# Folding the output projection into the expert weights earlier, in another PSUM bank, with a new order of all stages

## The chip, the cores and the metric

The kernel runs on one core of a Trainium2 chip. The metric is the device time of one execution in microseconds (us), lower is better. The core has five engines that run side by side and meet only through semaphores: TensorE (PE, matrix products, writes PSUM), VectorE (DVE), ScalarE (ACT), GpSimd (POOL, which doesn't touch PSUM here) and SyncE (SP, which issues the DMAs). PSUM has 8 banks of 128 partitions x 512 float32.

## The reference

Two transformer layers on 8 sequences of 128 tokens, model width 128, float32. Cut to what matters:

```
x  = LN(x) attends over the context (77 rows), plus x           # front, "p1"
h  = LN(x)                                                      # "ln1"
Q, K, V = h @ q_w, h @ k_w, h @ v_w         # 16 heads, 4 numbers each in Q, K and V
A  = softmax(Q K^T / 2) V                   # [tokens, 64]
mla = A @ o_w[0:64] + o_b
probs = softmax(mla @ router_w + router_b); keep the top 2 of 8 experts
moe = sum_e combine_e * (gelu(mla @ w1[e] + b1[e]) @ w2[e] + b2[e])
x  = x + h + 0.3 * moe                      # then a second layer: "p4" (cross attention), "p5" (expert 7)
```

`mla` is used only as a factor of `router_w` and of `w1[e]`. The kernel never forms it: it computes `o_w @ w1[e]` for the eight experts ("fold", 128x2048 in all) and `o_w @ router_w` ("fr"), and multiplies `A` with these. `o_b` rides along as one more row.

## The kernel before

**Stages and order.** Every engine runs its own function with named stages. A table of some 800 words, `plan`, gives one order of all stages; `run` walks it on each engine and executes the stages which that engine has. So the order of a word against words of the same engine is the order of the engine's queue, which is strict; between engines only semaphores count. A word like `s1:2,0` is a stage with its arguments (sequence 2, group 0).

**Front.** The 8 sequences go through it in three units u of 2, 3 and 3. For each: `p1_stats`, `p1_norm`, `p1_T` (transpose on PE), `p1_scores`, `p1_soft` (exponentials on ACT), `p1_pT`, `p1_av` (context attention, then added to x by DVE L824), `p1_ln`, `p1_norm1`, `p1_T2`, `p1_qk` (Q, K, V), `p1_split`: Q and K are cut into three bfloat16 parts `part` (L836, L839). The attention needs these parts stacked in groups of partitions, in the tiles `kst` and `qbd`. For unit 0 that is done on the chip: `rows` multiplies `part` with selection matrices (`own`, `aoT`, which POOL makes in `z_sel`), ACT copies the result to `kst`, DVE copies 16 pieces on to `qbd` (L860). For units 1 and 2 it goes through memory: `p1_parts:u` on SP writes `part` out in six DMAs (L374, L377), waits for them, and reads them back in eight (L391, L392). `stack_in1` counts these.

**Attention, per sequence b and group g of 4.** `s1:b,g` are four products (scores, PE) of which DVE takes the negated maxima (L866). When all four groups are there, `msp:b` (POOL) splits the maxima, and `mT:b` transposes them (PE, then ACT L647). `s2:b,g` computes the scores again, transposed and with the maximum subtracted (two 128x512 products); ACT exponentiates them to `pexp` (L654); `av:b,g` multiplies with the values in bank 5 (even b) or 6 (odd b). `un:b`, `den:b`, `norm:b` divide by the sum; `den` uses bank 4.

**The fold.** `oT` transposes `o_w` (L1247, bank 4) and copies it to `woT`; it waits for `part_ok` 3, since bank 4 is the bank of unit 2 in the front. `fold:k` (k = 0..3) is one float32 product of 128x512 for two experts (two passes in the trace) into bank 4, which ACT copies over `w1s` (L686). Each fold waits for `ln_ok` k+1, and `den:b` for the fold before it, as both use bank 4. After folds 0 and 1, `dw:0` on SP copies the rows of the folded weights to the other half of each group of partitions (the code then multiplies in two precisions), and after folds 2 and 3 `dw:1`; POOL splits them in `w1:e`.

**Fillers.** `warm:n` (n times) and `hot:b,k` are products of constants, 128x256 in bfloat16, read by nobody (`ps<-ones` in the trace, 70 in all): 46 `warm` into bank 1 and 24 `hot` into banks 5 and 6, of which 22 stand between `s1:0,1` and `mT:0`, and 2 after `s1:2,0`.

**The rest.** After the attention the experts follow in three units (`m1`, `gelu`, `m2`, `acc`), interleaved with the second layer (`p4_*`, `p5_*`). ACT's copies of zeros to `qbd` (`a_q`), `vpad` (`a_v`) and `kst` (`a_k`) clear tiles, as POOL's `z_q` and `z_v` do.

Of the kernel before, what the change touches and what calls it, by code (L numbers as in the profile page):

```python
# [52 lines left out]
def build(nc, x, ctx_in, q_w, q_b, k_w, k_b, v_w, v_b, o_w, o_b, router_w, router_b, w1, b1, w2, b2,  # L53
          w_sim, b_sim, w_qv, b_qv, wr, fw1, fb1, fw2, fb2, out):
    stack = ExitStack()
    with stack:  # L56
# [228 lines left out]
        def stages_of(text):  # L285
# [9 lines left out]
            warm:4 p1_stats:0 warm:5 a_q:0 warm:2 z_mask warm:1 z_sel:0 warm:6 p1_stats:1 p1_ctx:0 p1_norm:0 warm:2 p1_T:0 warm:1  # L295
            p1_stats:2 warm:1 p1_norm:1 p1_ctx:1 p1_scores:0 p1_parts:1 warm:1 p1_soft:0 warm:1 p1_norm:2 warm:1 p1_T:1 selg
            warm:1 p1_pT:0 p1_scores:1 warm:3 p1_av:0 warm:1 a_q:1 p1_soft:1 z_q:0 p1_ctx:2 warm:1 p1_pT:1 warm:4 p1_ln:0
            p1_norm1:0 warm:1 setup z_identb p1_av:1 a_q:2 p1_T2:0 p1_T:2 warm:1 z_wqk warm:2 p1_qk:0 z_sel:1 a_v:0 p1_ln:1 warm:1
            p1_split:0 p1_norm1:1 warm:2 p1_scores:2 warm:4 p1_v:0 rows:0 rows:1 rows:2 p1_T2:1 z_q:1 rows:3 p1_qk:1 p1_split:1
            s1:0,0 a_q:3 p1_soft:2 s1:0,1 a_v:1 a_k p1_v:1 hot:0,0 hot:0,1 hot:0,2 hot:0,3 hot:0,4 hot:0,5 hot:0,6 hot:0,7 hot:0,8  # L300
            hot:0,9 hot:0,10 hot:0,12 hot:0,14 hot:0,19 s1:0,2 z_v:0 p1_pT:2 s1:0,3 hot:0,15 hot:0,17 hot:0,20 p1_av:2 z_v:1
            p1_parts:2 hot:0,11 hot:0,13 hot:0,16 hot:0,18 hot:0,21 mT:0 p1_ln:2 s1:1,0 p1_norm1:2 s1:1,1 s2:0,0 s2:0,1 s1:1,2
            p1_T2:2 av:0,0 s1:1,3 s2:0,2 p1_split:2 z_v:2 p1_qk:2 s2:0,3 p1_v:2 mT:1 av:0,1 av:0,2 s1:2,0 hot:1,1 hot:1,0 s1:2,1
            s2:1,0 s2:1,1 z_msp oT av:0,3 s1:2,2 un:0 s1:2,3 s2:1,2 s2:1,3 s1:3,0 fr av:1,0 z_selg msp:0 av:1,1 s1:3,1 z_den den:0
            s1:3,2 mT:2 av:1,2 av:1,3 msp:1 s1:3,3 s2:2,0 s2:2,1 norm:0 un:1 fold:0 s1:4,0 s2:2,2 av:2,0 mT:3 s2:2,3 un:2 av:2,1
            den:1 av:2,2 msp:2 av:2,3 ctxw:0 s2:3,0 s1:4,1 ctxw:1 s2:3,1 fold:1 s2:3,2 s1:4,2 s2:3,3 msp:3 den:2 av:3,0 av:3,1
# [1157 lines left out]
```

## Time and profile before

| | |
|---|---|
| median of 3 runs | 163.97 us (163.97 to 164.05) |
| profiled execution, its own time | 165.47 us |
| its span, first to last instruction | 163.7 us |
| PE busy, matmuls | 151.9 us, 93% |
| DVE busy | 109.9 us, 67% |
| ACT busy | 107.3 us, 66% |
| POOL busy | 42.7 us, 26% |

The profile is of one execution. It is 1.50 us above the median, and its span leaves out 1.77 us of its own time. Busy times are sums over the span; an engine's share of it says nothing about which stage waits for which.

### The profile page before, as it was taken

The numbers are of one execution on the slowest core, as the hardware profiler recorded it, in microseconds if no ns is written. First come the engines' busy times: TensorE is split into PE (matmuls) and PEld (weight loads), VectorE is DVE, ScalarE is ACT, GpSimd is POOL, SyncE is SP. The second block draws the span as 40 slices with busy tenths as digits, with TensorE's granted clock in tenths as the row PEclk, the third lists the DMA queues.
The fourth block names the chain that finished last, engine by engine and source line by source line (L and its number), as shares of the span: only waits on it lengthen the run. The fifth ranks groups of instructions, "written<-read, shape, count | busy, mean of one in ns | idle before, by whom it ended". The sixth has DMA issues, their size and how long they took to land.

```text
span 163.7 us, 4023 instructions
## 1 busy us (share of the span) xinstructions
PE 151.9 (93%) x1336; PEld 122.5 (75%) x1336; DVE 109.9 (67%) x408; ACT 107.3 (66%) x238; POOL 42.7 (26%) x126
## 2 busy tenths in 40 slices
PE   7898997897999999999999999999899989999891
PEld 5686885554745566656899799998799969779780
DVE  2746999977844785661087827986747897687744
ACT  3668687463586677789759635555954595665580
...
DMA packets 11071, 8.02 MB, mean 49 GB/s; under 512 B 1867, under 2 KB 10155, under 8 KB 11051
## 3 DMA queue, kind: packets, MB, share of 16 engines
...
q8 instruction: 11, 0.18, 0.5%
q14 instruction: 9, 0.07, 0.1%
HBM read 5.26 MB, written 1.70 MB: 43 GB/s over the span
## 4 chain that ended last, share of the span: by engine, by line
PE 46%; issue 27%; DVE 9%; DMA 5%; SPq 4%; POOL 4%; ACT 2%; ACTq 1%; POOLq 1%; DVEq 0%
PE ps L1082 44%; DMA qbd<-scratch_q 2%; DMA x<-in_x_dram 2%; DVE qbd L860 2%; POOL rstd L568 2%; DVE stats L771 2%; DMA scratch_k<-part 1%; SPq L374 1%; POOL xn L562 1%; SPq L391 1%; PE ps L1120 1%; ACTq L56 1%; POOL f_lo L538 1%; SPq L377 1%; DVE vpad L979 1%
## 5 line engine op out<-in xcount | busy, mean ns | idle before, releaser
L704 ACT ACTIVATE vpad<-ps,b1o 128x256 f32<-128x256 f32 (+1 forms) x48 | 23.6, 543 | 16.0 <-PE ps L1082 15.9
L1082 PE MATMUL ps<-w2s,vpad 128*128 128x128 f32 x256 | 31.5, 276 | 0.2 <-DVE vpad L979 0.2
L1082 PEld LDWEIGHTS ps<-w2s,vpad 128*128 128x128 f32 x256 | 30.0, 192 | 0.8 <-issue 0.5
L866 DVE TENSOR_REDUCE nmax<-ps 128x4 f32<-128x512 f32 x32 | 21.2, 685 | 8.9 <-PE ps L1082 8.8
L979 DVE SCALAR_TENSOR_TENSOR vpad<-ps,comb,vpad 128x128 f32<-128x128 f32 x64 | 18.5, 342 | 10.4 <-PE ps L1082 10.1
L654 ACT ACTIVATE pexp<-ps 128x512 f32<-128x512 f32 x32 | 18.4, 595 | 8.3 <-PE ps L1082 7.8
L1082 PE MATMUL ps<-ao,w_lo 128*128 128x256 f32 (+1 forms) x48 | 16.4, 356 | 0.0
L568 POOL TENSOR_TENSOR rstd<-veps,power 128x2 f32<-128x2 f32 (+1 forms) x6 | 4.9, 809 | 39.4 <-DVE veps L781 39.4
L1082 PEld LDWEIGHTS ps<-kst,qbd 128*128 128x128 bf16 x128 | 8.6, 98 | 8.7 <-issue 5.4
L1082 PE MATMUL ps<-ao,w_hi 128*128 128x256 f32 (+1 forms) x48 | 14.5, 318 | 0.0
L1082 PE MATMUL ps<-ones 128*128 128x256 bf16 x70 | 13.2, 327 | 1.1 <-DVE nil L766 1.1
L1082 PE MATMUL ps<-kst,qbd 128*128 128x128 bf16 x128 | 11.8, 219 | 2.4 <-DMA qbd<-scratch_q 1.3
L1082 PE MATMUL ps<-qbd,kst 128*128 128x512 bf16 x32 | 12.2, 381 | 0.2 <-ACT mT L647 0.2
L1082 PE MATMUL ps<-mT,selg 128*128 128x512 bf16 x32 | 12.1, 379 | 0.0
L1082 PE MATMUL ps<-pexp,vpad 128*32 128x128 f32 x256 | 10.4, 279 | 0.0
L1082 PEld LDWEIGHTS ps<-ao,w_lo 128*128 128x128 f32 x48 | 9.1, 189 | 1.5 <-issue 0.6
L1082 PEld LDWEIGHTS ps<-ones 128*128 128x128 bf16 x70 | 8.1, 121 | 2.5 <-DVE nil L766 1.1
L562 POOL TENSOR_TENSOR xn<-vpad,bqv 128x256 f32<-128x256 f32 (+1 forms) x3 | 2.7, 913 | 27.6 <-DVE vpad L979 27.6
L1082 PEld LDWEIGHTS ps<-ao,w_hi 128*128 128x128 f32 x48 | 9.1, 189 | 0.5
L752 ACT ACTIVATE qbd<-ps,cols 128x256 f32<-128x256 f32 (+1 forms) x12 | 6.3, 545 | 3.8 <-PE ps L1082 3.7
L1082 PEld LDWEIGHTS ps<-pexp,vpad 128*32 128x32 f32 x256 | 6.0, 109 | 3.6 <-issue 1.3
L1082 PE MATMUL ps<-f2s,qbd 128*128 128x128 f32 x64 | 8.3, 278 | 0.0
...
## 6 DMA issues: line engine op xcount, KB each, us to landing
...
```

The lines of the kernel that those rows point to most:

```text
L56: with stack:
L374: sp.dma_start(scratch_q[:, r:r + m, c], part[0:LAT, q:q + 1, c].to_broadcast([LAT, m, n])).then_inc(s[f"parts_out{u}"], 16)
L562: pool.tensor_tensor(out=x2b[:, seqs(u), :], in0=x2[:, seqs(u), :], in1=bqv[:, :].unsqueeze(1).to_broadcast([P, UNITS[u][1], D]), op=ALU.a ...
L568: pool.tensor_tensor(out=rstd[:, i, seqs(u)], in0=veps[:, i, seqs(u)], in1=power[:, seqs(u)], op=ALU.pow).then_inc(s[f"ln{i}_rstd"], 1)
L654: act.activation(pexp[:, n % 3, :], ps[:, 2 + n % 2, :], ACT.Exp, scale=KPH ** -0.5).then_inc(s["p_ok"], 1)
L704: act.activation(hT[:, k % 2, c, 0:n], ps[:, h1_bank(k, c), 0:n], ACT.Gelu, bias=b1o[:, e, c:c + 1]).then_inc(s["gelu_ok"], 1)
L752: act.activation(gT[:, c, toks(u)], ps[:, (bank_a, bank_b)[c % 2][u], 0:UNITS[u][1] * S], ACT.Gelu, bias=cols[:, R_FB1 + c:R_FB1 + c + 1]) ...
L771: a = did(dve.bn_stats(stats[:, i, b, :], src[:, b, :]))
L860: last = dve.tensor_copy(qbd[r, g, j, 0:FRONT[0][1] * S], kst[r, g, T // 2:T])
L866: dve.tensor_reduce(nmax[:, b, g, :], ps[:, n % 2, :].rearrange("p (j t) -> p j t", t=S), axis=AX.X, op=ALU.max, negate=True).then_inc(s[" ...
L979: dve.scalar_tensor_tensor(out=x2[:, a + i, :], in0=ps[:, 2 + k % 2, i * D:(i + 1) * D], scalar=comb[:, a + i, e:e + 1], in1=x2[:, a + i, ...
L1082: return nc.tensor.matmul(dst, lhsT, rhs, start=start, stop=stop)
```

## The change

`EARLY = 4`: all four folds are computed in bank 5, before the first weighted values `av:0,0` are, in place of the 22 `hot` fillers. For that `o_w` is transposed in the front, into bank 0, right after the transposed router weights of the second layer, and its DMA counts on the semaphore `wr_in`. Fold k waits for the copy of fold k-1 (`w1o_ok`), the first for bank 5 to be free; `rows:0`, which uses bank 0, waits for `woT_ok`; `av:0,0` waits for the fourth copy. `den:b` then waits for no fold that is late. The table `plan` is written anew throughout; it has 53 `warm` and no `hot`.

```diff
+EARLY = 4
-            rows:3 p1_qk:1 p1_split:1 s1:0,0 a_q:3 p1_soft:2 s1:0,1 a_v:1 a_k p1_v:1 hot:0,0 hot:0,1 hot:0,2 ...
+            rows:2 p1_parts:2 rows:3 p1_qk:1 a_v:1 fold:0 p1_split:1 s1:0,0 s1:0,1 p1_soft:2 fold:1 p1_pT:2 s1:0,2 s1:0,3 a_k
+            p1_av:2 p1_v:1 fold:2 mT:0 p1_ln:2 s1:1,0 s1:1,1 fold:3 s2:0,0 s2:0,1 ...
...
-            sp.dma_start(wo[:, :], o_w[0:LAT, :]).then_inc(s["w1_in"], 16)
+            sp.dma_start(wo[:, :], o_w[0:LAT, :]).then_inc(s["wr_in"], 16)
...
# ACT: wo_T reads ps[:, 0, 0:LAT] instead of ps[:, 4, 0:LAT]; in fold(k):
-   ps[:, 4, :]
+   ps[:, 5 if k < EARLY else 4, :]
...
# PE: hot(0, k) and av(0, 0) in addition
+                    pe.wait_ge(s["w1o_ok"], EARLY)
# PE: rows_of(0)
-                    pe.wait_ge(s["wr_ok"], 1)
+                    pe.wait_ge(s["woT_ok"], 1)
# PE: den(b), 1 <= b <= 4
-                    pe.wait_ge(s["w1o_ok"], b)
+                    pe.wait_ge(s["w1o_ok"], min(b + EARLY, HALF))
             def wo_T():
-                pe.wait_ge(s["w1_in"], 64)
-                pe.wait_ge(s["part_ok"], NFRONT)
-                nc.tensor.transpose(ps[:, 4, 0:LAT], wo[:, :], ident[0:LAT, 0:LAT]).then_inc(s["woT_ps"], 1)
+                pe.wait_ge(s["wr_in"], 48)
+                pe.wait_ge(s["wr_ok"], 1)
+                nc.tensor.transpose(ps[:, 0, 0:LAT], wo[:, :], ident[0:LAT, 0:LAT]).then_inc(s["woT_ps"], 1)
             def fold(k):
-                pe.wait_ge(s["ln_ok"], k + 1)
-                mm(ps[:, 4, :], woT[:, :, :, :].rearrange("p j a x -> p (j a x)"),
+                if k < EARLY:
+                    pe.wait_ge(s["woT_ok"], 1)
+                    pe.wait_ge(s["w1_in"], 48)
+                    if k:
+                        pe.wait_ge(s["w1o_ok"], k)
+                    else:
+                        av_bank_free(0)
+                else:
+                    pe.wait_ge(s["ln_ok"], k + 1 - EARLY)
+                mm(ps[:, 5 if k < EARLY else 4, :], woT[:, :, :, :].rearrange("p j a x -> p (j a x)"),
```

PE's queue behind Q, K and V of unit 1 (`wv,xT` x3), up to the scores of sequence 1 or a little further, before:

```order
L1082 MATMUL ps<-xT,wqk 128x384
L1082 MATMUL ps<-wv,xT 128x64 x3
L1082 MATMUL ps<-kst,qbd 128x128 x8
L1082 MATMUL ps<-ones 128x256 x14
L1082 MATMUL ps<-kst,qbd 128x128 x4
L1143 MATMUL ps<-ident,pr 77x128 x3
L1082 MATMUL ps<-kst,qbd 128x128 x4
L1082 MATMUL ps<-ones 128x256 x3
L1082 MATMUL ps<-ctxn,pT 128x128 x3
L1082 MATMUL ps<-ones 128x256 x5
L1082 MATMUL ps<-identb,xn 128x128 x4
L1082 MATMUL ps<-kst,qbd 128x128 x8
```

and now:

```order
L1081 MATMUL ps<-wv,xT 128x64 x3
L1081 MATMUL ps<-w1s,woT 128x512
L1081 MATMUL ps<-kst,qbd 128x128 x8
L1081 MATMUL ps<-w1s,woT 128x512
L1144 MATMUL ps<-ident,pr 77x128 x3
L1081 MATMUL ps<-kst,qbd 128x128 x8
L1081 MATMUL ps<-ctxn,pT 128x128 x3
L1081 MATMUL ps<-w1s,woT 128x512
L1081 MATMUL ps<-identb,xn 128x128 x4
L1081 MATMUL ps<-kst,qbd 128x128 x8
L1081 MATMUL ps<-w1s,woT 128x512
L1081 MATMUL ps<-qbd,kst 128x512
```

The 22 fillers (`ps<-ones`) are gone, and the four folds (`ps<-w1s,woT`) stand between the scores of sequences 0 and 1 (`ps<-kst,qbd`). The line numbers are those of each file; L1081 now is L1082 before.

PE's queue, from unit 1's transposed probabilities (`ident,pr`) to Q and K of unit 0 (`xT,wqk`), before:

```order
L1082 MATMUL ps<-ones 128x256
L1143 MATMUL ps<-ident,pr 77x128 x3
L1082 MATMUL ps<-ones 128x256 x5
L1110 MATMUL ps<-ident,rows 128x25
L1113 MATMUL ps<-ident,wrn 128x8
L1082 MATMUL ps<-ctxn,pT 128x128 x3
L1120 MATMUL ps<-ident,xn 128x128 x5
L1082 MATMUL ps<-ones 128x256 x3
L1082 MATMUL ps<-xT,wqk 128x256
```

and now:

```order
L1129 MATMUL ps<-ident,ctxn 128x77 x3
L1081 MATMUL ps<-ones 128x256 x2
L1144 MATMUL ps<-ident,pr 77x128 x3
L1081 MATMUL ps<-ones 128x256 x6
L1111 MATMUL ps<-ident,rows 128x25
L1114 MATMUL ps<-ident,wrn 128x8
L1081 MATMUL ps<-ones 128x256
L1121 MATMUL ps<-ident,xn 128x128 x2
L1250 MATMUL ps<-ident,wo 128x64
L1081 MATMUL ps<-ctxn,pT 128x128 x3
L1081 MATMUL ps<-ones 128x256 x2
L1121 MATMUL ps<-ident,xn 128x128 x3
L1081 MATMUL ps<-xT,wqk 128x256
```

The product `ctxn,pT` x3 is `p1_av:1`, the context attention of unit 1. It stood right behind the transposed router weights (`ident,wrn`). Now a filler, the two transposes of unit 0 (`p1_T2:0`, `ident,xn` x2) and the transposed `o_w` (`ident,wo`) stand ahead of it.

ACT's queue at the softmax of units 0 and 1 (`pr,rs`), before:

```order
L591 ACTIVATE xT<-ps 128x384
L630 ACTIVATE pT<-ps 77x256
L596 ACTIVATE qbd<-nil 128x4x192
L625 ACTIVATE pr,rs<-ps,mx 128x77 x3
L617 ACTIVATE ctxT<-ps 128x231
L630 ACTIVATE pT<-ps 77x384
```

and now:

```order
L590 ACTIVATE xT<-ps 128x384
L595 ACTIVATE qbd<-nil 128x4x192
L629 ACTIVATE pT<-ps 77x256
L624 ACTIVATE pr,rs<-ps,mx 128x77 x3
L616 ACTIVATE ctxT<-ps 128x231
L629 ACTIVATE pT<-ps 77x384
```

The copy of zeros to `qbd` (`a_q:1`) was behind the copy of the transposed probabilities of unit 0 (`pT<-ps 77x256`) and is ahead of it.

POOL's queue changes too: the second selection matrix, `z_sel:1` (tile `own`), which stood ahead of `z_q:1` and `z_v:0`, now stands behind them and behind `z_den`, `z_msp`, `z_mask` and `z_selg`. `z_selg` waits for a small reduction on DVE (`selg`), which now stands behind `p1_norm1:0`. DVE's four small operations of `oT` moved into the front, ahead of `p1_av:1`.

## Rows read from the trace of the kernel before

**Rows 1.** The chain that ended last, in order of time: start us, us, what
```profile
10.58 0.91 PE ps L1082 x6
...
14.82 0.88 PE ps L1082 x6
...
15.73 0.88 DVE x L824 x3
...
26.05 0.67 SPq L374
...
29.36 2.02 DMA scratch_k<-part
...
34.29 3.53 DMA qbd<-scratch_q
...
37.87 1.70 PE ps L1082 x14
39.57 0.20 PE ps L1247
```
**Rows 2.** Busy time by stretch; the columns are in the first line
```profile
core 0: us, PE busy (x) PEld busy (x) DVE busy (x) ACT busy (x) POOL busy (x), PEclk, DMA share, GB/s
24.00:37.87 13.87, 10.78 (x111) 7.44 (x108) 12.07 (x35) 8.68 (x20) 4.39 (x18) 1.00 0.40 86
37.87:76.06 38.19, 38.03 (x457) 23.38 (x457) 23.85 (x71) 28.20 (x67) 14.59 (x49) 1.00 0.33 74
```
**Rows 3.** Timeline of PE: start us, us, line, operation, idle before, releaser
```profile
35.93 0.64 PE L1082 MATMUL ps<-pexp,vpad 128*32 128x128 f32 x16
...
38.10 0.38 PE L1082 MATMUL ps<-ones 128*128 128x256 bf16 x2
...
38.54 0.38 PE L1082 MATMUL ps<-qbd,kst 128*128 128x512 bf16 x1
...
38.98 0.38 PE L1082 MATMUL ps<-qbd,kst 128*128 128x512 bf16 x1
...
45.42 1.02 PE L1082 MATMUL ps<-w1s,woT 128*128 128x512 f32 x2
46.28 0.39 PE L1082 MATMUL ps<-kst,qbd 128*128 128x128 bf16 x4
```
**Rows 4.** Fillers on PE in 1:3, 9.2:10, 10.6:11.4, 24:25.5: xcount, busy us, mean ns
```profile
L1082 PE MATMUL ps<-ones 128*128 128x256 bf16 x10 | 2.3, 418 | 1.1 <-DVE nil L766 1.1
...
L1082 PE MATMUL ps<-ones 128*128 128x256 bf16 x2 | 0.8, 417 | 0.0
...
L1082 PE MATMUL ps<-ones 128*128 128x256 bf16 x1 | 0.3, 273 | 0.0
...
L1082 PE MATMUL ps<-ones 128*128 128x256 bf16 x14 | 1.7, 272 | 0.0
```
**Rows 5.** Timeline of ACT
```profile
10.83 0.83 ACT L596 ACTIVATE qbd<-nil 128x768 f32<-128x768 f32 x1
...
46.48 0.60 ACT L686 ACTIVATE w1s<-ps 128x512 f32<-128x512 f32 x1
```
**Rows 6.** Timeline of DVE
```profile
7.38 0.84 DVE L786 SCALAR_TENSOR_TENSOR xn<-x,mv,rstd 128x128 f32<-128x128 f32 x3
...
14.44 0.61 DVE L786 SCALAR_TENSOR_TENSOR xn<-x,mv,rstd 128x128 f32<-128x128 f32 x2 [0.60 <-ACT rstd L587]
...
18.99 0.88 DVE L786 SCALAR_TENSOR_TENSOR xn<-x,mv,rstd 128x128 f32<-128x128 f32 x3
...
40.50 2.00 DVE L866 TENSOR_REDUCE nmax<-ps 128x4 f32<-128x512 f32 x3 [0.26 <-PE ps L1082]
```
**Rows 7.** Timeline of POOL
```profile
7.43 0.74 POOL L450 MEMSET own<- 128x768 uint32 x1
8.31 1.92 POOL L456 TENSOR_SCALAR_AFFINE_SELECT own<-own 128x64 bf16<-128x64 bf16 x6
...
26.41 0.36 POOL L472 MEMSET vpad<- 128x48 f32 x4 [7.56 <-ACT vpad L596]
```

More of the change, by code:

```diff
@@ L294, in build @@
         plan = stages_of("""
[L295 to L306, printed above, removed]
@@ L327, in build @@
-            p5_prob:1 p5_router:2 p5_f1:2,0 p5_f1:2,1 p5_end:0 p5_f1:2,2 p5_f1:2,3 p5_f2:1,1 p5_end:1 p5_prob:2 p5_f2:2,0 p5_exp:2
-            p5_f2:2,1 p5_end:2
+            warm:1 z_sel:0 warm:1 z_identb a_q:0 warm:1 z_den p1_stats:0 warm:9 p1_ctx:0 p1_stats:1 warm:5 p1_norm:0 warm:2 z_wqk
+            warm:1 p1_T:0 warm:3 p1_stats:2 p1_ctx:1 p1_norm:1 p1_scores:0 warm:2 p1_soft:0 warm:1 p1_norm:2 p1_T:1 warm:2 a_q:1
+            warm:1 p1_pT:0 warm:3 p1_parts:1 p1_scores:1 warm:1 p1_av:0 warm:2 p1_soft:1 p1_ctx:2 warm:2 p1_pT:1 warm:2 z_msp
@@ new lines, in build @@
+            warm:2 p1_ln:0 p1_norm1:0 warm:2 setup selg warm:1 a_q:2 p1_T2:0 oT a_q:3 p1_av:1 warm:2 p1_T:2 p1_qk:0 warm:1 p1_ln:1
+            warm:2 z_q:0 warm:1 p1_split:0 p1_v:0 warm:1 p1_scores:2 a_v:0 warm:1 p1_norm1:1 warm:1 rows:0 z_mask rows:1 p1_T2:1
+            rows:2 p1_parts:2 rows:3 p1_qk:1 a_v:1 fold:0 p1_split:1 s1:0,0 s1:0,1 p1_soft:2 fold:1 p1_pT:2 s1:0,2 s1:0,3 a_k
+            p1_av:2 p1_v:1 fold:2 mT:0 p1_ln:2 s1:1,0 s1:1,1 fold:3 s2:0,0 s2:0,1 p1_norm1:2 s1:1,2 s1:1,3 p1_T2:2 z_v:0
@@ new lines, in build @@
+            p1_split:2 z_q:1 z_selg av:0,0 p1_qk:2 s2:0,2 z_sel:1 mT:1 s2:0,3 z_v:1 av:0,1 av:0,2 s2:1,0 ctxw:0 s1:2,0 s1:2,1
+            av:0,3 s2:1,1 s1:2,2 s2:1,2 s1:2,3 un:0 msp:0 p1_v:2 fr s1:3,0 s2:1,3 s1:3,1 av:1,0 av:1,1 den:0 mT:2 s1:3,2 s1:3,3
+            av:1,2 z_v:2 s2:2,0 un:1 msp:1 av:1,3 s2:2,1 s2:2,2 s1:4,0 av:2,0 s2:2,3 av:2,1 norm:0 den:1 s1:4,1 mT:3 av:2,2 av:2,3
+            un:2 s1:4,2 s2:3,0 s1:4,3 s2:3,1 msp:2 den:2 s1:5,0 s2:3,2 msp:3 s2:3,3 dw:0 av:3,0 msp:4 av:3,1 msp:5 norm:1 un:3
@@ L685, in fold @@
                 act.wait_ge(s["w1o_ps"], k + 1)
-                act.activation(w1s[:, 2 * k:2 * k + 2, :].rearrange("p e f -> p (e f)"), ps[:, 4, :], ACT.Copy).then_inc(s["w1o_ok"], 1)
+                act.activation(w1s[:, 2 * k:2 * k + 2, :].rearrange("p e f -> p (e f)"), ps[:, 5 if k < EARLY else 4, :], ACT.Copy).then_inc(s["w1o_ok"], 1)
             def router(h):
```

52 lines of the change are left out of this document (29 added, 23 removed).

## The prediction

> **What bounds the kernel now.** I read the chain of waits first, then busy time by stretch, then the timeline of each engine in the front. The chain [rows 1] shows three parts. Until 26.05 the front's own work sets the time: context attention, normalisation, the splitting of Q and K for unit 1. From 26.05 to 37.87 it is the trip through memory of these parts: six writes issued by SP, 2.02 us until the last lands, eight reads, 3.53 us until the last of them lands. From 37.87 the chain is PE. The stretches say the same [rows 2]: from 24 to 37.87 PE is busy 10.78 of 13.87 us, DVE 12.07 and ACT 8.68; from 37.87 to 76.06, PE 38.03 of 38.19, DVE 23.85 and ACT 28.20. So work taken from PE behind 37.87 is worth its full price. Work put on PE between 24 and 37.87 may cost nothing as long as its wait for the reads remains: PE is through with what it can do at 35.93 + 0.64 = 36.57 [rows 3] and waits 1.30 us, and on the way there it runs 22 fillers.
>
> **The sum is made against the profiled execution**, whose own time of 165.47 us is its span of 163.7 and 1.77 around it. The median is 1.50 lower; I carry the difference over to it unchanged. A measurement of this kernel can tell about 0.2%, 0.33 us, from no change.
>
> **What leaves PE behind 37.87.** A fold is two passes of 128x512 in float32. From the start of one at 45.42 to the next instruction at 46.28 it takes 0.86 us [rows 3]. Four folds: 3.44 us. The transpose of o_w took 0.20 us [rows 1]. The two fillers behind s1:2,0 go; 14 fillers in 1.7 us [rows 4] are 0.12 each, so 0.24. One s2 (two products, 38.54 to 38.98, 0.44 us) stands in the new order ahead of the first s1 that waits for the reads, and behind it before. Together 3.44 + 0.20 + 0.24 + 0.44 = 4.32 us less for PE to do once the reads have landed. ACT's share of the folds is four copies of 0.60 [rows 5], which also leave this stretch; ACT and DVE have more than a quarter of it free [rows 2], so PE stays its bound.
>
> **What they cost where they go.** Between 24 and 37.87 PE has 3.1 us idle [rows 2] and 22 fillers of 0.12, 2.6 us: 5.7 us, against 3.44 of folds and 0.44 of the s2. By total it fits with 1.8 to spare. By order, each fold waits for the copy of the one before it, and DVE (12.07 of 13.87 busy) releases the scores one by one, so a fold can come in at the wrong moment. Walking through the new order with these durations, PE ends what stands ahead of s1:2,0 about 0.85 us ahead of the landing of the reads. I put this at zero. If the cover is gone: before, PE ended this work at 36.57. Were fillers to have filled only idle time and each fold to push everything behind it, it would end 3.44 + 0.44 later plus the shift of the front below, that is 2.6 us behind the landing, which is the upper end; below zero it can't be, for SP's trip sets the landing.
>
> **The front gets later.** The start of SP's trip hangs on the chain up to 26.05. Three edits bear on it.
> (1) Between the first transpose of unit 0 and p1_pT:0 there are nine fillers and were six. At that time a filler takes long: ten in 2.3 us, mean 418 ns and still 417 between 9.2 and 10, against 273 behind 10.6 and 272 later (14 in 1.7) [rows 4]. The start-to-start times are 0.22 to 0.23 and 0.12 us for the 256 columns: the lower and the upper of the array's two levels, 1.2 and 2.4 GHz, though the granted clock of the page reads full throughout (as in [rows 2] for later stretches). Two or three fillers at the lower level and three more at the upper level ahead of p1_scores:1, which was on the chain at 10.58 [rows 1] and had some idle before it: 0.3 to 1.0, I take 0.75 us. ACT's copy of zeros ahead of the copy of p1_pT:0 (0.83 us [rows 5]) runs beside the same fillers and needs nothing of its own.
> (2) p1_av:1 on PE started at 14.82 and DVE's x followed at 15.73 [rows 1]. Now the transposes of unit 0 are ahead of it, and wait for DVE's norm, which ended at 14.44 + 0.61 = 15.05 [rows 6]. With the shift of (1) that is 15.80; the second transpose and that of o_w take some 0.3, the six passes 0.88 [rows 1], DVE starts about 17.05 instead of 15.73 + 0.75: 0.55 more.
> (3) POOL makes the selection matrix late: 0.74 and 1.92 us [rows 7], behind a cast that waits for DVE's reduction behind norm. I allow 0.9 for these two, small operations both: 15.80 + 0.9 + 2.7 is 19.4. The products of rows need it when the split of unit 0 is done, which was at 18.99 [rows 6] (start of the norm behind it) and will be at 20.3. Hidden, with 0.9 to spare; each us beyond that would be a us.
> Folds in this place don't delay the split of unit 1: it waits for DVE, which has its 16 copies to do first. Sum of the front: 0.75 + 0.55 = 1.3 us, with ends 0.3 (the fillers were covered by waits) and 2.2 (all six at the lower level, 1.3, and 0.9 in (2)).
>
> At this place a rule speaks against the change. The row first: three norms of DVE, each with two inputs in SBUF, took 0.84 us at 7.38 while POOL worked without a pause, and 0.88 at 18.99, in POOL's idle time of 7.56 us ahead of 26.41 [rows 6, 7]: POOL costs DVE nothing here. The Trainium skill, GPSIMD Engine Reference, Specifications, has it that VectorE and GpSimd share their SBUF interfaces, and that VectorE instructions with two SBUF inputs contend with GpSimd. Now POOL works on the matrix until 19.4, beside DVE's chain. By the rule the norms and splits there might lose up to their own 0.9 us and the result would be near 162.4; by the rows it is nothing, and I go by the rows.
>
> **Stalls in the attention.** With folds gone from between the stages, PE reaches the scores sooner, and waits for DVE: three maxima take 2.00 us [rows 6], 0.65 each. In the new order s1:3,2 and s1:3,3 come right behind mT:2, where DVE also has p1_v:2 and fr to do; PE waits there some 0.5 us by my walk. Bounds: 0, and 1.5 (two such maxima more, or the second trip through memory being late). I take 0.5. The later reorderings are of work that PE does without a pause, and I put them at zero, within 0.4 each way.
>
> **Sum.** -4.32 + 1.3 + 0.5 = -2.5 us. Profiled span 161.2, its own time 163.0, median 161.5 us. With all ends: -4.0 to -0.1 and, with the lost cover, above zero.
>
> **Rivals.**
> A. The front isn't delayed, since fillers stood in waits: -4.32 + 0.3 + 0.3 = -3.7, 160.2 us. For it: some idle on PE before 10.58. Against it: p1_av:1 is itself on the chain and now has three instructions ahead of it.
> B. The folds outlast the trip. Half of the upper end of 2.6: -2.5 + 1.3 = -1.2, 162.8 us. For it: the maxima, POOL's split and ACT's copies are a chain with PE in it, and fold 2 and 3 stand inside it. Against it: 1.8 us to spare by total.
> C. Slower: the fillers kept the array at its upper level, and without them it falls to the lower when PE waits for the first fold's copy or for the reads. For it: at the start of the kernel the level rose only between 10 and 10.6 us, although PE had been running fillers and products since 1.1 [rows 4], so that a fall is dear. Against it: the folds occupy PE longer than the fillers did, and the wait of 1.30 us did no harm before. Price: if it falls at the start of the stretch that PE bounds and takes the same 9.4 us or so to return, half of that is lost, 4.7 us: 161.5 + 4.7 = 166.2 us. It decides from 5 us at the lower level on, where 2.5 us are lost.
> D. The change doesn't do what it says: a fold waits for something late (w1 in SBUF, woT) and the folds fall behind 37.87. Then 3.44 come back: 164.9. Against it: but for the reads of unit 1, the chain behind 10 us has no wait for a DMA that loads weights.
>
> **Chances.** Forecast 0.60, A 0.14, B 0.18, C 0.05, D 0.03. Of B a tenth part ends within 0.2% or above, as does a small part of the forecast. Faster by over 0.2% (below 163.64): 0.88; within: 0.05; slower: 0.07. The range that leaves out 2 in 10 reaches from A to a little beyond B: 160.1 to 163.2.
>
> **What would show it.** Right: in the chain the reads of unit 1 land near 39.2 and PE's first product behind them starts there after an idle of about 0.9 us; four `w1s,woT` between 24 and 33; from there to the first m1 (76.06 before, 38.19 us long) the stretch is some 3.8 us shorter, with PE busy all but 0.5 us. Front: DVE's x of unit 1 at 17.0. Wrong: no idle ahead of s1:2,0 (B); fillers or products with the long start-to-start times behind 24 us (C); POOL's last piece of `own` behind 20.3 (POOL sets the front); an experts' stretch that is longer by more than 0.4 us. The prediction falls if the median is above 163.2 or below 160.1.

## Result and profile after

The changed kernel takes 162.43 us (median of 17 runs, 161.35 to 163.70), the kernel before 164.14 beside it (17 runs, 163.74 to 165.75). The ratio is 0.9884, 95% interval [0.9857, 0.9912]: 1.9 us less (1.7 by the two medians). 161.5 was predicted, 160.1 to 163.2 the range. The profiled execution took 162.74, its span 161.0; that of before 165.47 and 163.7. Ratios are of fast runs alone, here and below; left out are one run each of kernels 3 (281.38 us), 6 (168.09) and 8 (164.27, the one that was profiled).

The chain of the changed kernel (start us, us, what), the places that answer to [rows 1]:

```profile
14.81 0.88 PE ps L1081 x6
15.72 0.88 DVE x L823 x3
...
25.97 0.67 SPq L373
...
29.30 2.03 DMA scratch_k<-part
...
32.98 1.54 SPq L390
...
35.40 2.45 DMA qbd<-scratch_q
37.90 4.12 PE ps L1081 x50
```

The reads of unit 1 are waited for until 37.90, against 37.87 in [rows 1]. I had expected 39.2. The front seems to stand where it stood. PE's timeline from the first fold to the first m1 (the last line), cut:

```profile
23.15 1.08 PE L1081 MATMUL ps<-w1s,woT 128*128 128x512 f32 x2
...
25.00 1.10 PE L1081 MATMUL ps<-w1s,woT 128*128 128x512 f32 x2 [0.33 <-ACT w1s L685]
...
28.23 1.02 PE L1081 MATMUL ps<-w1s,woT 128*128 128x512 f32 x2
...
30.30 1.08 PE L1081 MATMUL ps<-w1s,woT 128*128 128x512 f32 x2
...
36.74 0.39 PE L1081 MATMUL ps<-qbd,kst 128*128 128x512 bf16 x1
...
37.90 0.62 PE L1081 MATMUL ps<-kst,qbd 128*128 128x128 bf16 x8 [0.77 <-DMA qbd<-scratch_q]
...
72.97 0.48 PE L1081 MATMUL ps<-ao,w_lo 128*128 128x512 f32 x1
```

All four folds are done before the reads land (two of them start before SP's first write at 25.97), and PE still waits 0.77 us for the reads behind them (0.9 was foretold). The busy time by stretch (columns as in [rows 2]) shows the trade: from 24 us to the reads 11.68 us of PE for 10.78, behind them 34.21 for 38.03.

```profile
24.00:37.90 13.90, 11.68 (x100) 6.94 (x100) 11.91 (x33) 10.13 (x24) 2.02 (x12) 1.00 0.38 86
37.90:72.97 35.07, 34.21 (x437) 21.16 (x444) 24.68 (x68) 25.59 (x61) 14.74 (x49) 1.00 0.36 81
```

From the reads to the first m1 it is 35.07 us and was 38.19: 3.12 less, 3.8 were foretold. From the first m1 to the end it is 161.0 - 72.97 = 88.03 and was 163.7 - 76.06 = 87.64: 0.39 more. Taken at face value the two profiles say: front 0.0, attention -3.1, experts and the rest +0.4. The first of these three is misleading, as the experiments showed.

### The profile page after: what moved, and what is told of

Read it like the earlier page. It is cut to its first block, busy times and chain, and to the rows that moved or that the text cites. A ratio compares the mean times of both kernels' runs of the same rounds, so it can differ in the third digit from the quotient of the medians.

```text
span 161.0 us, 3987 instructions
## 1 busy us (share of the span) xinstructions
PE 149.2 (93%) x1311; PEld 119.7 (74%) x1319; DVE 110.1 (68%) x408; ACT 107.2 (67%) x238; POOL 42.6 (26%) x126
## 4 chain that ended last, share of the span: by engine, by line
PE 50%; issue 21%; DVE 9%; SPq 5%; DMA 5%; ACT 4%; POOL 3%; ACTq 1%; POOLq 1%; DVEq 0%
PE ps L1081 47%; DVE qbd L859 2%; DMA x<-in_x_dram 2%; SPq L390 2%; POOL rstd L567 2%; DMA qbd<-scratch_q 2%; DMA scratch_k<-part 1%; SPq L373 1%; DVE stats L770 1%; PE ps L1121 1%; POOL xn L561 1%; ACTq L57 1%; DVE nmax L865 1%; ACT L718 1%; SPq L376 1%
## 5 line engine op out<-in xcount | busy, mean ns | idle before, releaser
L1081 PE MATMUL ps<-w2s,vpad 128*128 128x128 f32 x256 | 31.8, 277 | 0.0
L1081 PEld LDWEIGHTS ps<-w2s,vpad 128*128 128x128 f32 x256 | 30.1, 192 | 0.8 <-issue 0.4
L1081 PE MATMUL ps<-ao,w_lo 128*128 128x256 f32 (+1 forms) x48 | 16.6, 358 | 0.7 <-ACT vpad L703 0.7
L1081 PE MATMUL ps<-ao,w_hi 128*128 128x256 f32 (+1 forms) x48 | 14.7, 318 | 0.0
L1081 PE MATMUL ps<-kst,qbd 128*128 128x128 bf16 x128 | 11.5, 219 | 1.5 <-DMA qbd<-scratch_q 0.8
L1081 PEld LDWEIGHTS ps<-kst,qbd 128*128 128x128 bf16 x128 | 8.5, 98 | 5.6 <-issue 3.2
L1081 PE MATMUL ps<-qbd,kst 128*128 128x512 bf16 x32 | 12.2, 382 | 0.3
L1081 PE MATMUL ps<-pexp,vpad 128*32 128x128 f32 x256 | 11.0, 280 | 0.3
L1081 PE MATMUL ps<-ones 128*128 128x256 bf16 x53 | 10.2, 328 | 1.1 <-DVE nil L765 1.1
L1081 PEld LDWEIGHTS ps<-ao,w_lo 128*128 128x128 f32 x48 | 9.1, 189 | 1.9 <-issue 1.1
L549 POOL CAST xn<-nmax 128x16 bf16<-128x16 f32 x8 | 1.7, 217 | 30.2 <-DVE nmax L865 30.2
L1081 PEld LDWEIGHTS ps<-pexp,vpad 128*32 128x32 f32 x256 | 5.8, 108 | 5.0 <-issue 2.7
L1081 PEld LDWEIGHTS ps<-ao,w_hi 128*128 128x128 f32 x48 | 9.1, 189 | 0.5
L1081 PE MATMUL ps<-mT,selg 128*128 128x512 bf16 x24 | 9.1, 379 | 0.0
L1081 PE MATMUL ps<-f2s,qbd 128*128 128x128 f32 x64 | 8.3, 278 | 0.0
```

The lines of the kernel that those rows point to most:

```text
L549: a = did(pool.tensor_copy(m[:, :, 0, :], v))
L1081: return nc.tensor.matmul(dst, lhsT, rhs, start=start, stop=stop)
```

## Experiments

T1 is the prediction: attention is bound by PE, so each us of folds is worth a us there; they cost nothing in the trip; the front is later by two steps. The rivals: the folds do cost something in the trip; the relief is worth less than its PE time; the front isn't later at all. The first four kernels take the folds away, double them or put them back. Differences between experiments and the changed kernel are between ratios to the kernel before that ran on the same chip (before: 164.19, 164.24 and 164.35 in the three groups).

**1. Folds shrunk in the changed kernel.** Product and copy of each fold take 8 columns of 512.

```
-  act.activation(w1s[:, 2 * k:2 * k + 2, :] ..., ps[:, 5 ..., :], ACT.Copy)
+  act.activation(w1s[:, 2 * k, 0:8], ps[:, 5 ..., 0:8], ACT.Copy)
-  mm(ps[:, 5 ..., :], woT ..., w1s[:, 2 * k:2 * k + 2, :] ...)
+  mm(ps[:, 5 ..., 0:8], woT ..., w1s[:, 2 * k, 0:8])
```

Expected:

> The changed kernel with its four folds shrunk to 8 of 512 columns, both the product on TensorE and the copy on ScalarE (it leaves out the fold of the output weights into the experts' first weights, all but 8 columns). T1, the theory of the prediction: the folds lie in the time in which SP brings unit 1's parts back from memory, TensorE is idle there before p1_qk:1 as it is, so the last read still starts at about 35.4 and ends that stretch at 37.9: same as the changed kernel, 162.4, within 0.4. Rival B (the folds delay p1_qk:1 or the stretch): up to 4 x (0.86 of product + 0.60 of copy) comes off the front, 1 us faster or more.

Measured: 163.73 us, ratio 0.9966 [0.9933, 0.9999]; 1.3 us slower than the changed kernel, with less work. Neither theory had this. Busy time by stretch of 2 us in its profile:

```profile
24.00:26.00 2.00, 1.16 (x5) 0.67 (x5) 1.97 (x4) 1.64 (x11) 0.00 (x0) 1.00 0.00 0
26.00:28.00 2.00, 1.34 (x13) 1.22 (x14) 2.00 (x5) 0.86 (x1) 0.00 (x0) 0.89 0.44 87
28.00:30.00 2.00, 1.44 (x12) 1.35 (x12) 1.54 (x9) 0.18 (x1) 1.15 (x8) 0.50 0.75 153
30.00:32.00 2.00, 2.00 (x13) 1.42 (x12) 1.97 (x9) 1.16 (x4) 0.00 (x0) 0.50 0.27 55
32.00:34.00 2.00, 2.00 (x14) 1.45 (x11) 1.43 (x5) 1.19 (x2) 0.00 (x0) 0.50 0.66 168
34.00:36.00 2.00, 1.79 (x16) 0.96 (x14) 0.63 (x2) 0.59 (x2) 0.85 (x4) 0.90 0.43 100
```

The granted clock (the column behind POOL) is 0.50 from 28 to 34 us: the array runs at 1.2 GHz, after some 4 us in which PE was busy 1.16 and 1.34 of 2 us. A score product with `mT` takes 0.63 us in that stretch, and 0.38 behind it. So this run says nothing on what the folds cost in the trip, and no other run has them away at the full clock. It says what they do there besides: **they are the fillers now**. Mechanism C of the prediction exists; full-size folds stay clear of it, as the 1.00 in the rows after shows. Not all of the 1.3 us is lost at the lower level itself: in the profile the first product behind the reads starts 0.63 us later (38.53 for 37.90), and the other 0.63 up to the first m1 (74.23 for 72.97) come behind it, at a granted clock of 1.00, 0.46 of them a wait for POOL's split of the maxima (`xn`) at 61.47. That wait comes back in kernels 8 and 9.

**2. Folds doubled in the changed kernel.** Each product of a fold runs twice.

```
+  mm(ps[:, 5 ..., :], woT ..., w1s[:, 2 * k:2 * k + 2, :] ...)
   mm(ps[:, 5 ..., :], woT ..., w1s[:, 2 * k:2 * k + 2, :] ...).then_inc(s["w1o_ps"], 1)
```

Expected:

> The changed kernel with each of its four fold products run twice into the same bank (same output). Adds 4 x 0.86 to 1.08 = 3.4 to 4.3 us of TensorE work between 23 and 32 us. T1: the profile after shows 0.77 us idle before the first instruction that waits for the read, 0.33 us of idle before the second fold, and waits before the third and the fourth that p1 work partly fills; so some 1 to 1.5 of the 3.4 is covered and 2 to 2.5 us show, 164.4 to 164.9. Rival F (the window is loose, TensorE could do all of it): within 0.4 of 162.4. If TensorE had no slack there at all: 165.8 or more.

Measured: 165.04 us, ratio 1.0044 [1.0011, 1.0077], 2.6 us slower than the changed kernel for 4 x 0.86 = 3.44 us of work. T1's 2 to 2.5 is about right, "the window is loose" falls. What was covered is 0.8 us, uncertain by some 0.7 (both ratios have an interval), which agrees with the idle time of 0.77 ahead of the reads. So the folds fit with some 0.8 us to spare in that profile, and rival B was that near.

**3. Folds shrunk in the kernel before.** The same edit as in 1, in the middle of attention.

Expected:

> The kernel before with its four folds, in the middle of attention, shrunk to 8 of 512 columns in product and copy (it leaves out the fold, all but 8 columns). T1 (attention is bound by TensorE, so a fold is worth its whole 0.86): 4 x 0.84 = 3.4 us faster than before, 160.7. Rival E (the relief is worth less there than its TensorE time, because the softmax chain on VectorE and ScalarE sets the pace in places): 1.5 to 2.5 us faster, 161.6 to 162.6, and TensorE's waits in the attention grow by the rest.

Measured: 162.91 us, ratio 0.9918 [0.9888, 0.9947], 1.3 us faster, less than either theory had. A shrunk fold isn't free: it takes 0.14 to 0.28 us from its start to the next instruction's, and PE's busy time behind the reads is 35.56 us where it was 38.03, so 2.5 us left it, not 3.4. The stretch from the reads to the first m1 is 36.71 us (36.55 to 73.26) and was 38.19, 1.5 shorter. PE's timeline of this kernel shows new waits in [ ], where [rows 2] had 38.03 busy of 38.19:

```profile
36.55 0.40 PE L1082 MATMUL ps<-kst,qbd 128*128 128x128 bf16 x4 [1.20 <-DMA qbd<-scratch_q]
...
49.15 0.38 PE L1082 MATMUL ps<-qbd,kst 128*128 128x512 bf16 x1 [0.17 <-ACT pexp L654]
...
53.38 0.38 PE L1082 MATMUL ps<-kst,qbd 128*128 128x128 bf16 x4 [0.46 <-DVE nmax L866]
...
54.68 0.39 PE L1082 MATMUL ps<-qbd,kst 128*128 128x512 bf16 x1 [0.19 <-ACT mT L647]
...
62.52 0.38 PE L1082 MATMUL ps<-kst,qbd 128*128 128x128 bf16 x4 [0.36 <-DVE nmax L866]
```

1.18 us of waits in four places stand where 2.5 us of folds stood. In the old order PE was busy throughout *because* the folds filled the gaps that maxima and exponents leave. A busy share of 99% was read as "PE is the bound"; it only says that nothing else showed. This is rival E, though 1.3 us is a little below the 1.5 to 2.5 that it was given. (The profiled run took 164.25 us, 1.34 above this kernel's median: from 134 to 138 us its granted clock fell to 0.61 and 0.54. That is far behind the attention and touches nothing read here.)

The first row holds a second finding. The front has not one changed instruction against the kernel before, yet its reads are waited for until 36.55, not 37.87. The fillers of either profile tell why. Before, and then this kernel:

```profile
5.13 0.63 PE L1082 MATMUL ps<-ones 128*128 128x256 bf16 x2
6.85 0.63 PE L1082 MATMUL ps<-ones 128*128 128x256 bf16 x2
8.51 0.84 PE L1082 MATMUL ps<-ones 128*128 128x256 bf16 x3
```

```profile
4.94 0.38 PE L1082 MATMUL ps<-ones 128*128 128x256 bf16 x2
6.14 0.38 PE L1082 MATMUL ps<-ones 128*128 128x256 bf16 x2
7.28 0.49 PE L1082 MATMUL ps<-ones 128*128 128x256 bf16 x3
```

From 5.13 on, two fillers take 0.63 us and three 0.84 in the one execution, 0.38 and 0.49 in the other: the array's upper level came at about 4.9 us here, and between 10 and 10.6 in the profile of before [rows 4]. The profiled execution of before was one of a late rise: 165.47, where the median is 164.14. Kernel 4 below, again with before's front, also has an early rise (two fillers in 0.38 us from 6.49 on).

**4. Folds alone moved.** Before's order of all other stages; the transpose of o_w (into bank 5) and the folds replace the 22 fillers, and GpSimd makes z_den in its idle time.

```
-  s1:0,0 a_q:3 p1_soft:2 s1:0,1 a_v:1 a_k p1_v:1 hot:0,0 ... hot:0,19 s1:0,2 z_v:0 p1_pT:2 s1:0,3 hot:0,15
-  hot:0,17 hot:0,20 p1_av:2 z_v:1 p1_parts:2 hot:0,11 ... hot:0,21 mT:0
+  s1:0,0 a_q:3 oT fold:0 p1_soft:2 s1:0,1 a_v:1 fold:1 a_k p1_v:1 s1:0,2 z_v:0 p1_pT:2 s1:0,3 fold:2
+  p1_av:2 z_v:1 p1_parts:2 fold:3 mT:0
```

Expected:

> The kernel before in its own order, with nothing but the folds moved: the transpose of o_w (into the bank of the first weighted values) and the four folds take the place of the 22 fillers there; z_den earlier on GpSimd, where it idles. Same output. T1 with the full price (attention bound by TensorE, front as before): 3.64 off, and 0.4 lost in the window: 160.9. T2, formed after the run with small folds in the kernel before (TensorE had 2.4 us less work there, 1.3 us came off, and 1.2 us of new waits for VectorE's maxima and ScalarE's exponents stood in its place): half the relief or a little more, 1.8 to 2.2 off, 162.0 to 162.4; the rest of the gain needs the changed order of attention.

Measured: 164.91 us, ratio 1.0034 [1.0005, 1.0062]. **The folds' move by itself makes the kernel slower**, by 0.1 to 0.6%. T1 and T2 both had it faster, and both were wrong. Its timeline of PE, all waits between the trip and the first m1:

```profile
37.58 0.40 PE L1083 MATMUL ps<-kst,qbd 128*128 128x128 bf16 x4
38.64 0.39 PE L1083 MATMUL ps<-ones 128*128 128x256 bf16 x2 [0.67 <-DVE vpad L850]
50.82 0.38 PE L1083 MATMUL ps<-qbd,kst 128*128 128x512 bf16 x1 [0.29 <-ACT pexp L655]
55.05 0.38 PE L1083 MATMUL ps<-kst,qbd 128*128 128x128 bf16 x4 [0.60 <-DVE nmax L867]
56.34 0.39 PE L1083 MATMUL ps<-qbd,kst 128*128 128x512 bf16 x1 [0.19 <-ACT mT L648]
64.18 0.38 PE L1083 MATMUL ps<-kst,qbd 128*128 128x128 bf16 x4 [0.50 <-DVE nmax L867]
73.19 0.49 PE L1083 MATMUL ps<-un,selden 128*128 128x128 f32 x2 [0.43 <-ACT un L661]
75.64 0.48 PE L1083 MATMUL ps<-ao,w_lo 128*128 128x512 f32 x1
```

Two things. The folds outlast the trip: its first product behind the reads starts at 37.58 with no idle time, against 36.55 in 3, so 1.0 is lost (rival B, in the old order; the transpose of `o_w` stands in the trip here as well, and PE waits 0.56 us for its copy). And from 37.58 to 75.64 it is 38.06 us, hardly less than before's 38.19, with 2.68 us of waits in six places in the room of 3.44 of folds.

**5 and 6. Folds put back late in the new order.** The early transpose stays. In 5 the first three folds stand at most two stages of PE ahead of the `den` that needs their copy, in 6 four to six stages ahead; the fourth is further ahead in both.

```
-  a_v:1 fold:0 p1_split:1      (and three more)
+  a_v:1 hot:0,0 ... hot:0,3 p1_split:1
-  av:1,3 s2:2,1      av:2,3 un:2      av:3,2 av:3,3      w1:0 s2:4,1
+  av:1,3 fold:0 s2:2,1      av:2,3 fold:1 un:2      av:3,2 fold:2 av:3,3      w1:0 fold:3 s2:4,1      (6)
```

Expected of 5:

> The changed kernel's order and its early transpose of the output weights, but the four folds put back into the middle of attention, one after each of norm:0, s2:3,1, norm:2 and un:4, in the old bank; four fillers stand where each fold stood (16 of the 22 that stood there before). Same output. T1: the fold's place is worth 4 x 0.86 = 3.4 us, so 162.4 + 3.4 = 165.8, slower than the kernel before by the front's 0.8 and the changed order. Rival G (much of the gain or loss is in the order of the rest and the folds' place is worth less, 2 us or under): 164.4 or under, about the kernel before.

Expected of 6:

> The changed kernel's order with the four folds in the middle of attention again, in the old bank, but each some four to six stages ahead of the den that waits for its copy (the earlier run had them right ahead of it, and TensorE waited 1.9 us for ScalarE's copies). Four fillers stand for each fold in the window. Same output. Price of the folds' place in this order, T1: 3.44 of TensorE and little else, 165.9. T2, after the two runs in the old order (2.4 us less work brought 1.3, folds moved alone brought nothing): the order of attention decides how much of it shows; in an order made without them they cost more than their 3.44, because copies and maxima come late, 166.5 to 168.

Measured: 5 takes 168.52 us, ratio 1.0248 [1.0200, 1.0297], and 6 takes 166.32, ratio 1.0098 [1.0065, 1.0130]. In 5 PE waits 1.9 us for three copies of the folds, a fault of my order. In 6 hardly any wait is left; PE's timeline shows one between 37 us and the first m1:

```profile
56.60 0.46 PE L1081 MATMUL ps<-un,selden 128*128 128x128 f32 x2 [0.20 <-ACT w1s L685]
```

Against the changed kernel, 6 is 1.0098 - 0.9884 = 0.0214, or 3.5 us, slower: the 3.44 of the folds. Its first m1 is at 76.46 (the changed kernel's 72.97), 3.49 later. T1 had 165.9, T2 166.5 and more: the difference of the ratios (162.43 + 3.5) is T1's, the median of 166.32 is nearer to T2's lower end. The two profiles side with T1. So in the new order the folds' place is worth about its full PE time.

| | folds in attention | folds in the trip |
|---|---|---|
| old order | 164.14 (1) | 164.91 (1.0034) |
| new order | 166.32 (1.0098) | 162.43 (0.9884) |

Either part alone makes the kernel slower, by 0.6 and 1.6 us; both together make it 1.9 faster. The whole time mixes the front in, though. The same table for the stretch from PE's first product behind the reads to the first m1, in us, with PE's busy time:

| | folds in attention | folds in the trip |
|---|---|---|
| old order | 38.19, 38.03 busy | 38.06, 35.26 busy |
| new order | 38.94, 38.62 busy | 35.07, 34.21 busy |

In the old order 2.8 us of busy time leave PE and 0.1 comes off the stretch, in the new one 4.4 leave and 3.9 come off. Kernel 6's loss is not all attention: against the old order with an early rise its profile loses 0.75 there, 1.0 ahead of it (37.52 for kernel 3's 36.55) and 0.3 behind the first m1, some 2 us where the ratio has 1.6. In kernels 5 and 6 the trip is 16 fillers long instead of 22, and the level fell in their profiles for some of it (granted clock 0.57 from 28 to 32 us in 6), which may hold some tenths of their time.

**7 to 12. The front.** All profiles in the new order start SP's first write at 25.7 to 26.1 us; the two profiles in the old order with an early rise have 24.84 and 24.99. That is some 0.9 us. I tried to get it back by undoing, one by one and together, what I had held responsible.

```
7   ... setup selg p1_av:1 warm:1 a_q:2 p1_T2:0 oT a_q:3          (p1_av:1 first, step 2 undone)
8   ... warm:2 p1_stats:2 p1_ctx:1 ... p1_T:1 / warm:1 p1_pT:0 a_q:1 p1_parts:1 p1_scores:1
                                                                  (six fillers less, step 1 undone)
9   7 and 8
10  VectorE: "oT": wo_T  ->  "av": lambda b, g: wo_T() if (b, g) == (0, 3) else None
11  7 and 10
12  7 and 10, and z_mask z_sel:1 on GpSimd, ahead of z_v:0        (step 3 undone)
```

Expected of 7:

> The changed kernel with p1_av:1 put back ahead of p1_T2:0 and of the transpose of o_w, as it stands before (step 2 of the front undone; same output). The profiled kernel before with small folds has x of unit 1 on VectorE at 14.51 us, all four profiles of the changed order at 15.48 to 15.72. T1 (the front of the changed kernel is later by two steps, and the profile of before only hid that, since its own front ran late that time): x of unit 1 at 15.0, and 0.5 us faster than the changed kernel, 161.9. Rival H (the front isn't later, the difference of the profiles is chance): within 0.3 of 162.4.

Expected of 8:

> The changed kernel with two fillers instead of three ahead of p1_ctx:1, none ahead of a_q:1 and none between p1_pT:0 and p1_scores:1, six fillers less in all, three of them on the way to scores:1 (step 1 of the front undone; same output). T1: x of unit 1 at 14.9 instead of 15.5, and about 0.7 us faster, 161.7. Rival H (the front isn't later): within 0.3 of 162.4. Rival C (fewer fillers let the array's level rise later or fall): 163 or more, with long fillers after 7 us.

Expected of 9:

> The changed kernel with both steps of the front undone (same output): p1_av:1 ahead of p1_T2:0 and oT, and six fillers less. T1: x of unit 1 at 14.5 as in the profile of before with small folds, the first instruction that waits for unit 1's read at 36.7 instead of 37.9, and 1.2 us faster than the changed kernel, 161.2. If the two overlap (both only wait for the same thing): 161.7. Rival I (the window cannot give it back, since TensorE's own row of work up to there is 0.77 short of full): 161.7 too, with no idle time of TensorE before that read.

Expected of 10:

> The changed kernel with VectorE's four instructions of stage oT (own, lower, upper, signs; 14.34 to 15.62 us in its profile) moved behind the first two maxima of the second batch's third group, some 22 us later; same output. In the changed kernel they stand right ahead of VectorE's x of unit 1, at 15.72. T3, formed after the runs that undid steps 1 and 2 of the front without any gain: these four hold VectorE, and p1_av:1 on TensorE, which ends at about 15.7 too, is as late; either alone hides the other. So this alone brings nothing: 162.4 within 0.3, x of unit 1 at 15.6. Rival J (VectorE alone sets it, TensorE's product was only late because nothing asked for it): 0.6 or more faster.

Expected of 11:

> Both at once: p1_av:1 ahead of p1_T2:0 and oT, and VectorE's four instructions later. Same output. T3: x of unit 1 at 15.0, its statistics right behind it, the split of unit 0 done at 17.9; but the products of rows need GpSimd's selection matrix too, ready at 18.37, so they start at 18.4 instead of 18.9, and SP's first write at 25.5 instead of 26.0: 161.9. If GpSimd's matrix doesn't hold (its wait comes earlier than the profile shows): SP at 25.0, 161.4.

Expected of 12:

> The same, and GpSimd's selection matrix for Q (z_sel:1) made ahead of the first zeros and ones of V, where it is ready at 13.7 instead of 18.37. Same output. T3: products of rows at 17.9 as in the kernel before, SP's first write at 25.0, the last read of unit 1 landed at 36.8, and 1.0 us faster than the changed kernel: 161.4. Rival I (TensorE's own work up to there fills the time, as the run with doubled folds showed only 0.8 us of cover): TensorE starts s1:2,0 at 37.1 to 37.3 without idle time, and it brings 0.5: 161.9.

| kernel | us | ratio [95%] | DVE x of unit 1 | rows start | SP's first write | PE behind the reads | first m1 |
|---|---|---|---|---|---|---|---|
| changed | 162.43 | 0.9884 [0.9857, 0.9912] | 15.72 | 18.93 | 25.97 | 37.90 | 72.97 |
| 7 | 162.33 | 0.9882 [0.9833, 0.9931] | 15.02 | 19.04 | 26.07 | 37.55 | 72.62 |
| 8 | 162.54 | 0.9866 [0.9819, 0.9913] | 15.74 | 18.95 | 25.98 | 37.77 | 74.55 |
| 9 | 162.73 | 0.9884 [0.9836, 0.9932] | 14.85 | 18.89 | 25.93 | 37.12 | 73.12 |
| 10 | 162.75 | 0.9900 [0.9864, 0.9937] | 15.51 | 18.73 | 25.77 | 37.53 | 73.04 |
| 11 | 162.43 | 0.9871 [0.9831, 0.9910] | 14.90 | 18.72 | 25.75 | 37.17 | 72.69 |
| 12 | 162.73 | 0.9884 [0.9845, 0.9923] | 14.88 | 18.70 | 25.73 | 37.58 | 73.36 |
| 4 (old order) | 164.91 | 1.0034 [1.0005, 1.0062] | 14.66 | 17.95 | 24.99 | 37.58 | 75.64 |

None differs from the changed kernel by more than its uncertainty, which is some 0.8 us. x of unit 1 does come earlier in 7, 9, 11 and 12, by 0.7 to 0.9 us, and the products of `rows` and SP's first write hardly do. The timelines show what holds it each time. VectorE in the changed kernel, where x has no idle time ahead of it:

```profile
14.34 0.79 DVE L883 TENSOR_SCALAR own<-ones,cols 128x128 f32<-128x128 f32 x1
...
15.21 0.41 DVE L889 TENSOR_TENSOR signs<-upper,lower 128x1 f32<-128x1 f32 x1
15.72 0.87 DVE L823 SCALAR_TENSOR_TENSOR x<-ps,rr,x 128x128 f32<-128x128 f32 x3
```

VectorE in kernel 9, where x comes early and its statistics wait for the same instructions:

```profile
14.85 0.87 DVE L823 SCALAR_TENSOR_TENSOR x<-ps,rr,x 128x128 f32<-128x128 f32 x3 [0.48 <-PE ps L1081]
15.63 0.69 DVE L883 TENSOR_SCALAR own<-ones,cols 128x128 f32<-128x128 f32 x1
...
16.41 0.26 DVE L889 TENSOR_TENSOR signs<-upper,lower 128x1 f32<-128x1 f32 x1
16.59 0.67 DVE L770 BATCH_NORM_STATS2 stats<-x 128x6 f32<-128x128 f32 x3
...
17.53 0.45 DVE L835 SCALAR_TENSOR_TENSOR res<-ps,cols,part 128x256 f32<-128x256 f32 x1
```

VectorE in kernel 12, where `res` waits for ScalarE, and below it ScalarE in the same kernel:

```profile
17.31 0.48 DVE L835 SCALAR_TENSOR_TENSOR res<-ps,cols,part 128x256 f32<-128x256 f32 x1 [0.49 <-ACT part L634]
```

```profile
15.49 0.22 ACT L679 ACTIVATE woT<-ps 128x64 f32<-128x64 f32 x1
...
15.69 0.84 ACT L595 ACTIVATE qbd<-nil 128x768 f32<-128x768 f32 x1
16.42 0.49 ACT L590 ACTIVATE xT<-ps 128x384 f32<-128x384 f32 x1
16.79 0.48 ACT L634 ACTIVATE part<-ps,cols 128x256 bf16<-128x256 f32 x1
```

Three engines got some 1 us of extra work at the same place, side by side: PE the transposes ahead of p1_av:1; VectorE the four instructions of stage `oT`, from 14.34 to 15.62 (with p1_av:1 first they stand behind x and ahead of its statistics, 15.63 to 16.59); ScalarE the copies of `woT` and the zeros of a_q:3, 15.49 to 16.42, ahead of the split of unit 0. In kernel 4 ScalarE's `part` starts at 16.05 and VectorE's `res` at 16.56; with ScalarE's share alone left (12) they start at 16.79 and 17.31, still 0.75 later. Whoever removes one or two meets the third. So T1's account of the front failed in 7, 8 and 9, and T3's held in 10 and failed in 11 and 12, since it had left ScalarE out. The times alone settle less: the 1.2 us foretold for 9 and the 1.0 for 12 lie outside their intervals, the 0.5 to 0.7 for 7, 8 and 11 do not. That ScalarE's share is the last of them is read from the rows of 12; a kernel without it wasn't run. That fewer fillers bring nothing to the front is read from the profile of 8: x of unit 1, the rows and SP's first write stand where they stood, and x waits 0.65 us for PE's product.

Even so the gain would be bounded, in two ways. First, in 7, 9 and 11 PE has no idle time ahead of the first product behind the reads, and 0.48 us in 12: PE's own work in the trip is about as long as the trip. Second, what does arrive earlier is lost again behind it. In 9 that product starts 0.78 us before the changed kernel's, and the first m1 0.15 us after it. PE's wait, and POOL's in the same profile:

```profile
37.12 0.61 PE L1081 MATMUL ps<-kst,qbd 128*128 128x128 bf16 x8
...
60.36 0.40 PE L1081 MATMUL ps<-identb,xn 128*128 128x128 bf16 x4 [0.76 <-POOL xn L555]
```

```profile
56.92 0.40 POOL L528 CAST w_hi<-w1s 128x256 fp32r<-128x256 f32 x1 [1.61 <-DMA w1s<-w1s]
```

POOL's queue is strict: the split of the maxima for PE stands behind the split of the folded weights (`w1:0`, `w1:1`), and that waits for SP's copies of them (`dw:0`), which stand in SP's queue behind the trip of unit 2. That trip starts at 36.7 to 37.0 us in all of these kernels, whatever unit 1's front does. POOL doesn't wait there in the changed kernel (`w_hi` at 56.05); it waits 1.61 us in 9, 1.90 in 8, where PE then waits 1.53 us and the run is 164.27, and 1.23 in 1. In 10, 11 and 12 the moved instructions of VectorE stand among the maxima at about 39 us instead, and PE waits 0.32 us for a maximum behind them. Whether the late copies come from these edits or by chance, one profile each doesn't tell.

## Why the prediction was right, and where it wasn't

The number was right (161.5 against 162.43, within the range), its parts were partly wrong. Its terms were -4.3 (relief), +1.3 (front), +0.5 (stalls), 0 (rest). Part of it was luck: the sum gave a span of 161.2 for the profiled run, and 161.0 came, but from one profile to the other the front moved by 0.0 instead of +1.3, the attention by -3.1 instead of -3.8 and the rest by +0.4 instead of 0. These misses cancel. (The ends of the terms add up to -4.4 and -0.2, where the prediction has -4.0 and -0.1; the range was not made from them.)

**Folds in the trip cost nothing.** Right as far as the runs show, and its margin too: 0.85 us by my walk, 0.77 in the profile, 0.8 by the doubled folds. In the profiles of 7, 9 and 11 the margin is gone, though, and a run without folds at the full clock is missing. Rivals B and D didn't happen; B did in the old order (kernel 4). There the transpose of `o_w` stands in the trip too, so whether the new order of the trip's stages or the earlier transpose keeps the folds inside isn't shown.

**The front is 1.3 later.** Wrong against the profile that it was worked out from: x of unit 1 came at 15.72, not at 17.0, and the product behind the reads at 37.90, not at 39.2. Against an execution of the old order with an early rise it is about right in size, and half wrong in cause: that product starts at 36.55 there, so 1.35, of which SP's first write is 1.13 (24.84 to 25.97). By the profiles of 7 to 12 it is 0.6 to 1.2. Step 2 named p1_av:1 behind the transposes as the cause, and step 1 the fillers; the profile of 8 shows nothing of step 1, and step 2 is one of three parallel causes. I had followed `oT` on PE and left out what the same word does on VectorE and ScalarE. Step 3 was right: GpSimd's matrix was done at 18.37, expected at 19.4, and moving it (12) changed nothing.

**The relief is 4.3 because PE is the bound behind 37.87.** This is the step that failed, in its reason. The stretch of 38.03 busy in 38.19 was taken as proof. In the old order PE time that is taken away turns into waits by half (3) or almost wholly (4). Only since the same change reorders attention did the full price appear: 3.5 us in the new order (6). The changed kernel's timeline of PE shows one wait for a maximum between the reads and the first m1, of 0.18 us at 55.10, where kernel 4 has two of 0.60 and 0.50. The size in the prediction is thus about right for this change, and would have been wrong for the folds' move alone. The Trainium skill, Perfetto Trace Analysis, Identifying the Most-Contended Engine, warns that a high busy share of matmuls is no good measure of TensorE's headroom, and takes the share of its weight loads instead (with the share of peak arithmetic). By that the stretch reads 23.38 of 38.19 us [rows 2], 61%, below ScalarE's 28.20. Kernels 3 and 4 agree that 99% busy was no measure of what a relief brings. The share of weight loads doesn't tell the two orders apart either: it is 58% in the same stretch of kernel 6 (22.67 of 38.94), where the full price came off.

**Stalls +0.5 and rest 0.** Mis-sized. Attention got 3.12 shorter, not 3.82. PE's busy time there fell by 3.82 (38.03 to 34.21), not by 4.32, and the time without PE busy grew by 0.70 (0.16 to 0.86), not by 0.5. Both carry some uncertainty, since some of PE's records are absent from the trace. The experts' stretch is 0.4 longer, at the end of my 0.4 each way; all profiles in the new order have 87.9 to 88.0 there, the two in the old order whose level held 87.6 and 87.7. The longest new wait of PE there is 1.11 us for VectorE's `sc` at 128.3, against 0.18 at 131.4 before. With the front at +1.35 the three come to 1.35 - 3.12 + 0.39 = -1.4 us; the profiled execution of the changed kernel is 0.3 above its median, which makes the 1.7 between the medians.

**The base.** The sum was made against an execution 1.3 us above the median and carried over. By the profiles the gain is 163.7 - 161.0 = 2.7, by the runs 1.9; most of the difference is the late rise of before's profile, 1.3 us later in front than kernel 3's. Rows 4 showed when it rose, but from one execution no one can tell whether that is usual.

**The rule on GpSimd and VectorE.** Three norms of VectorE took 0.87 us at 19.36 in the profile after, beside GpSimd's zeros (busy from 18.26 to 19.77), and 0.88 before in its idle time [rows 6, 7]. The Trainium skill, GPSIMD Engine Reference, Specifications, expects contention of instructions with two SBUF inputs. None is seen here, but GpSimd's instructions beside these norms were all fills (`MEMSET`), which read nothing, so the trace doesn't test the rule for GpSimd instructions that read.
